# Counts of routed rows and the causal mask given to TensorE, and the turning of an expert's rows put into the down projection before it

## The reference

```python
# layer 0 attention: 16 heads of 16, key j visible from query i where j >= i
scores = jnp.where(j >= i, einsum(q, k) * attn_scale, -jnp.inf)
out = softmax(scores) @ v ; x = layernorm(x + out @ w_out + b_out)
# layer 0 experts: top 2 of 8 (the last is a no-op), at most cap = 512 rows per expert, in token order
sorted_indices = jnp.argsort(-expert_mask, axis=0)[:cap]
h = relu(einsum('ceh,ehi->cei', inputs, experts_inter))      # 7 experts, 256 -> 1024
out = einsum('cei,eih->ceh', h, experts_out) * in_w[..., None]
combined = zeros.at[used_idx].add(out) + x_flat * (noop_w * noop_mask)
# layer 1 attention: rms norm, rotary, sigmoid weights over all keys divided by their sum
# layer 1 experts: top 2 of 12 (the last 4 pass x through), silu, no cap, 256 -> 512
```

## Time and profile before

| what | value |
|---|---|
| median of three runs | 1659.26 us (1654.88 to 1662.66) |
| the profiled execution | 1661.06 us, span of its instructions 1659.5 us |
| PE, DVE, ACT, POOL busy | 83%, 55%, 42%, 30% of the span |
| one turn of layer 0 attention, mean of four | 61.9 us |
| one expert of layer 0 | 29.4 us |
| mean granted TensorE clock | 0.909 of full |

### The profile page before, as it was taken

One profiled execution on the slowest core, in us unless ns is written; L12 is line 12 of the kernel. 1 busy time (PEld: TensorE's weight loads), 2 busy tenths in 40 slices (PEclk: granted clock), 3 DMA queues, 4 the chain that ended last, 5 costly groups with the idle time before them and its releaser, 6 DMA issues.

```text
span 1659.5 us, 31170 instructions
## 1 busy us (share of the span) xinstructions
PE 1383.2 (83%) x10239; PEld 933.8 (56%) x10240; DVE 908.2 (55%) x3424; ACT 703.9 (42%) x984; POOL 495.6 (30%) x415
## 2 busy tenths in 40 slices
PE   3678898898888369999459999999998649999991
PEld 1245555555555346665325556555655448999991
DVE  1767888878886401111266766876753353434434
ACT  2145554554555111111036676767776312222223
POOL 4032344334334302122111122132312224444442
PEclk7799899999898679999779999999999769999996
DMA  6855536545513024333154647545645424444446
GB/s 168 215 107 109 116 107 133 119 111 122 120 27 116 13 71 122 107 83 83 38 113 87 121 89 149 119 93 116 133 102 148 144 85 64 71 72 71 71 63 215
DMA packets 119550, 174.71 MB, mean 105 GB/s; under 512 B 17624, under 2 KB 101618, under 8 KB 113281
## 3 DMA queue, kind: packets, MB, share of 16 engines
q1 hardware_dynamic: 96320, 148.05, 37.5%
q0 software_dynamic: 20400, 22.37, 8.6%
q10 hardware_dynamic: 2704, 2.70, 0.5%
HBM read 107.64 MB, written 72.69 MB: 109 GB/s over the span
## 4 chain that ended last, share of the span: by engine, by line
PE 55%; DVE 6%; issue 5%; ACT 4%; DMA 4%; POOL 1%; SPq 1%; POOLq 0%; DVEq 0%; ACTq 0%
PE ST L1865 7%; PE OT L769 7%; PE shared L1877 7%; PE ST L751 7%; PE ST L1324 6%; PE shared L1523 3%; PE OT L1332 3%; PE shared L1332 3%; ACT arena L890 3%; PE shared L800 3%; PE shared L1530 1%; PE shared L817 1%; DMA sum<-arena,block_to_row 1%; PE shared L781 1%; DVE scratch L1158 1%
## 5 line engine op out<-in xcount | busy, mean ns | idle before, releaser
L890 ACT ACTIVATE arena<-ST 128x1024 f32<-128x1024 f32 x416 | 412.9, 1025 | 217.9 <-PE ST L751 216.8
L751 PE MATMUL ST<-arena 96*128 96x256 bf16 (+2 forms) x1792 | 246.5, 272 | 41.8 <-DMA arena<-qk_parts 20.4
L769 PE MATMUL OT<-arena,v_aug 128*32 128x256 f32 (+1 forms) x3584 | 241.4, 384 | 5.7 <-POOL arena L1226 5.1
L751 PEld LDWEIGHTS ST<-arena 96*128 96x128 bf16 (+1 forms) x1792 | 151.0, 100 | 152.1 <-ACT arena L890 58.0
L1158 DVE CUSTOM_DVE_ANT_0 scratch<-shared,mask 128x512 bf16<-128x512 f32 (+3 forms) x293 | 135.6, 497 | 56.8 <-PE shared L865 51.8
L1972 POOL DMA_INDIRECT sum<-arena,block_to_row x71 | 111.2, 1566 | 170.9 <-DMA sum<-arena,block_to_row 118.4
L769 PEld LDWEIGHTS OT<-arena,v_aug 128*32 128x32 f32 x3584 | 92.5, 112 | 107.9 <-issue 67.4
L1877 PE MATMUL shared<-arena 128*128 x568 | 134.8, 381 | 0.0
L1226 POOL TENSOR_SCALAR_AFFINE_SELECT arena<-arena 128x512 f32<-128x512 f32 (+1 forms) x96 | 79.6, 834 | 172.2 <-ACT arena L890 172.2
L1694 POOL DMA_INDIRECT slot_x<-x_out,row_to x64 | 63.7, 995 | 165.7 <-DVE keep L1612 148.6
L1877 PEld LDWEIGHTS shared<-arena 128*128 128x128 f32 x568 | 103.0, 191 | 11.2
(11 more groups left out here) (232 smaller groups left out, 2378.8 us busy)
## 6 DMA issues: line engine op xcount, KB each, us to landing
arena<-qk_parts SPq DMA_DIRECT2D x224, 128.0 KB, 7.2
qk_parts<-qk_src SPq DMA_DIRECT2D x32, 384.0 KB, 2.6
arena<-qk_parts SPq DMA_DIRECT2D x32, 384.0 KB, 4.6
qk_parts<-qk_src SPq DMA_DIRECT2D x64, 192.0 KB, 3.0
arena<-slot_x SPq DMA_DIRECT2D x71, 130.0 KB, 2.4
arena<-qk_parts SPq DMA_DIRECT2D x32, 256.0 KB, 5.5
sum<-x_out SPq DMA_DIRECT2D x16, 512.0 KB, 3.0
arena<-in_experts_inter SPq DMA_DIRECT2D x7, 1024.0 KB, 5.1
```

The lines of the kernel that those rows point to most:

```text
L751: mm = pe.matmul(scores[:, i * 256 + at:i * 256 + at + nq], K[par][0:rows, h, kb * P:(kb + 1) * P], Q[par][0:rows, h, q0:q0 + nq], start=T ...
L769: mm = pe.matmul(OT[32 * i:32 * i + 32, q0:q0 + nq], v_aug[par][:, kb, g * GH + i, :], PT[n % RING][:, i, at:at + nq], start=(u == 0), sto ...
L890: act.activation(PT[n % RING][:, :, :], scores[:, :].rearrange("p (h n) -> p h n", h=GH), func, scale=ATT_SCALE).then_inc(L["exp"], 1)
```

## The change

The change has three parts.

1. **Counts.** `count_before` and `r_before` are gone. PE makes the counts from `r_mask` itself, in five matmuls: one with `before` over all four tiles, three with `ones_b` over the mask moved on by one, two and three tiles, and one that adds a carry from earlier sequences. VectorE sums the mask in one instruction (`count_rows`, at the start of `l3`) and adds it to the other of two carry buffers (`carry_on`). `l2` shrinks from 22 to 17 pieces in layer 0 and from 5 to none in layer 1, so that the mixed order moves by a few places.
2. **Mask.** After each fill of scores PE adds the mask on the diagonal 128 columns of every part, by a matmul of `mask_b` with the identity. VectorE then takes the maxima of the whole bank with one `tensor_reduce`; where a bank holds 384 + 128 columns it keeps four maxima by block, and `mc` gains two instructions that join them. The waits of `mx` for its own older fills and the scratch output are gone.
3. **Experts of layer 0.** The transposes for expert e+1 stand before tile 3 of the down projection of expert e. ScalarE's copy to `xgT` waits for the end of the up projection of e.

```diff
-N_ROUTE = {True: (3, 22, 11), False: (13, 5, 11)}
+N_ROUTE = {True: (3, 17, 11), False: (13, 0, 11)}
...
                 pe.wait_ge(L["rc"], k * chain_len + mask_at)
-                for t in range(TB):
-                    pe.matmul(bank[:, t * ne:(t + 1) * ne], before[:, :], r_mask[:, t, 0:ne],
-                              start=True, stop=False)
-                    mm = pe.matmul(bank[:, t * ne:(t + 1) * ne], ones_b[:, :], r_before[:, t, 0:ne],
-                                   start=False, stop=True)
-                mm.then_inc(ready, 1)
+                sums = bank[:, 0:TB * ne].rearrange("p (t e) -> p t e", t=TB)
+                pe.matmul(sums, before[:, :], r_mask[:, :, 0:ne], start=True, stop=False, skip_group_check=True)
+                for t in range(1, TB):
+                    pe.matmul(sums[:, t:TB, :], ones_b[:, :], r_mask[:, 0:TB - t, 0:ne], start=False, stop=False,
+                              skip_group_check=True)
+                pe.matmul(sums, ones_b[:, :], r_carry[k % 2][:, 0:ne].unsqueeze(1).broadcast_to([P, TB, ne]),
+                          start=False, stop=True, skip_group_check=True).then_inc(ready, 1)
...
-                            mm = pe.matmul(bank[:, at:at + S - qb * P], Q[par][0:SK, head, qb * P:(qb + 1) * P],
-                                           K[par][0:SK, head, qb * P:S], start=True, stop=True)
+                            pe.matmul(bank[:, at:at + S - qb * P], Q[par][0:SK, head, qb * P:(qb + 1) * P],
+                                      K[par][0:SK, head, qb * P:S], start=True, stop=False, skip_group_check=True)
+
+                        for _, _, at in FILLS[n % len(FILLS)]:
+                            mm = pe.matmul(bank[:, at:at + P], ident_b[:, :], mask_b[:, :], start=False, stop=True,
+                                           skip_group_check=True)
...
-        def count_before(dve, chain, ne):
-
-            yield from chain(dve.tensor_copy(r_before[:, 0, 0:ne], r_before[:, TB, 0:ne]))
-            for t in range(TB):
-                yield from chain(dve.tensor_tensor(r_before[:, t + 1, 0:ne], r_before[:, t, 0:ne], r_mask[:, t, 0:ne],
-                                        ALU.add))
+        def count_rows(dve, chain, ne):
+
+            chain.unwaited(dve.tensor_reduce(r_count[:, 0:ne], r_mask[:, :, 0:ne].rearrange("p t e -> p e t"),
+                                             AX_X, ALU.add))
+
+        def carry_on(dve, chain, ne, k):
+
+            chain.unwaited(dve.tensor_tensor(r_carry[(k + 1) % 2][:, 0:ne], r_carry[k % 2][:, 0:ne], r_count[:, 0:ne],
+                                             ALU.add))
...
-                            taken = dve.tensor_tensor_reduce(
-                                out=junk[n % 2][:, at:at + m], in0=bank[:, at:at + m], in1=mask[:, 0:m],
-                                scale=1.0, scalar=LOW, op0=ALU.add, op1=ALU.max, accum_out=mx[:, i:i + 1])
-                        taken.then_inc(free, 1)
+                        if fill == 2:
+                            dve.tensor_reduce(of_all[:, head:head + 2, 2], bank[:, :].rearrange("p (h n) -> p h n", h=2),
+                                              AX_X, ALU.max).then_inc(free, 1)
+                        elif fill % 3 == 0:
+                            dve.tensor_reduce(of_all[:, head + fill // 3:head + fill // 3 + 1, 0], bank[:, :].unsqueeze(1),
+                                              AX_X, ALU.max).then_inc(free, 1)
+                        else:
+                            dve.tensor_reduce(mx_blocks[:, head + fill // 3, :],
+                                              bank[:, :].rearrange("p (b n) -> p b n", n=P),
+                                              AX_X, ALU.max).then_inc(free, 1)
...
+                        chain.unwaited(dve.tensor_reduce(of_all[:, heads, 1], mx_blocks[:, heads, 0:3], AX_X, ALU.max))
+                        chain.step(dve.tensor_copy(of_all[:, heads, 3], mx_blocks[:, heads, 3]))
...
                 for t in range(TB):
+                    if t == TB - 1 and e + 1 < E0:
+                        turn_rows(e + 1)
...
         def b_act(act):
             def emit(e, par, half):
+                wait(act, b_up, e * MI)
```

More of the change, by code:

```diff
@@ L522, in build @@
         scratch = sb("scratch", [P, S])
-        junk = [scratch[:, i * (S // 2):(i + 1) * (S // 2)].bitcast(BF16) for i in range(2)]
+        mask_b = sb("mask_b", [P, P], BF16)
         mx = sb("mx", [P, NH * TB])
+        mx_blocks = sb("mx_blocks", [P, NH, TB])
         mx_rest = sb("mx_rest", [P, NH * TB])
@@ L541, in build @@
         r_mask = sb("r_mask", [P, TB, NEM], BF16)
-        r_before = sb("r_before", [P, TB + 1, NEM], BF16)
+        r_carry = [sb(f"r_carry{i}", [P, NEM], BF16) for i in range(2)]
+        r_count = sb("r_count", [P, NEM])
         row_to = [sb(f"row_to{i}", [P, TB, 2], I32) for i in range(2)]
@@ L1083, in a_route_dve @@
                 yield from chain(dve.tensor_tensor(r_mask[:, :, 0:ne], oh[0], oh[1], ALU.add))
-                yield from count_before(dve, chain, ne)
                 assert chain.n == MASK0, chain.n
@@ L1161, in emit @@
-                        taken.then_inc(free, 1)
-                    elif step == "mc":
-                        for i in (2, 1):
-                            banks.read(dve, turn, ("mx", (n + 1) * HALF_MX - i))
-                        chain = Chain(dve, L["mchain"], k * 8 + 4 * n)
+                        of_all = mx[:, :].rearrange("p (h b) -> p h b", b=TB)
+                        fill, head = n % len(FILLS), n // len(FILLS) * 2
+                        if fill == 2:
[8 more added lines that the diff above has]
+                                              AX_X, ALU.max).then_inc(free, 1)
+                    elif step == "mc":
+                        for b in range(banks.n):
+                            banks.read(dve, turn, ("mx", max(i for i in range(n * HALF_MX, (n + 1) * HALF_MX)
+                                                             if banks.place[turn.kind][("mx", i)][0] == b)))
+                        chain = Chain(dve, L["mchain"], k * 12 + 6 * n)
+                        heads = slice(n * HH, (n + 1) * HH)
+                        of_all = mx[:, :].rearrange("p (h b) -> p h b", b=TB)
+                        chain.unwaited(dve.tensor_reduce(of_all[:, heads, 1], mx_blocks[:, heads, 0:3], AX_X, ALU.max))
+                        chain.step(dve.tensor_copy(of_all[:, heads, 3], mx_blocks[:, heads, 3]))
@@ L1597, in c_route_dve @@
                 chain.n = MASK1
+                count_rows(dve, chain, ne)
                 dve.wait_ge(L["ex"], k * 2 + 2)
@@ L1843, in d_pe @@
             pe.wait_ge(LC["oe"], NB * NG)
-            pe.matmul(shared[0][:, 0:E1], ones_b[:, :], r_before[:, TB, 0:E1], start=True, stop=True
+            pe.matmul(shared[0][:, 0:E1], ones_b[:, :], r_carry[NB % 2][:, 0:E1], start=True, stop=True
                       ).then_inc(d_cnt, 1)
```

43 lines of the change are left out of this document (18 added, 25 removed).

## The result

The changed kernel takes 1663.68 us (median of 20 runs, 1658.4 to 1670.74) where the kernel before takes 1659.24 us (20 runs, 1653.31 to 1665.03). The ratio is 1.0029, with a 95% interval from 1.0017 to 1.0041. Run a second time, beside other kernels on one chip, it is 1.0024 (1.0007 to 1.0041). So the change costs 4 us, inside the 0.5% that were to be called no change, where 9 us of gain were forecast.

The account below looks back on a forecast made before the run. PE was taken to lead about 47 us of a layer 0 middle turn, VectorE about 15. Terms of -8.4, -0.9, -3.0, +15, -7.2 and -4.5 sum to -9.0 us: 1650 us (1643 to 1658; outer range 1634 to 1667).

Parts of the forecast that it names:

- counts, with the stall and the three ends: Six layer 0 turns -8.4 us, one slow count instruction -0.9, three uncovered last turns (two in layer 1) -3.0.
- masks and clock: Layer 0 attention: PE's added mask matmuls on the path +15 us, PE's clock falling less often -7.2 us.
- turned rows: Layer 0 experts: moved transposes remove PE's 0.74 us wait for ScalarE's copies at six borders, -4.5 us.
- order: Order of steps in the turns shifts by a place or so: 2 us either way, nothing in the sum.
- outer range of 1634 to 1667 us: Whole kernel: the forecast's wide range, leaving out the slow rival and the tail below the clock's.
- I had written 0.3: End of layer 1: sign that the row from mask to `ps` takes under 0.3 us.
- +15: Layer 0 attention: of 32 us of mask matmuls, 2.0 us a turn on the path, ends 6 and 32.
- 0.6 us a turn, in one stretch: VectorE-led stretch of a layer 0 turn: gain from cheaper whole-bank fills, 7 of which count there.
- PE pays for every mask: Rival, layer 0 attention: all 32 us of masks on the path, clock brings nothing; 1674 us, chance 0.12.
- The wait moves and the clock stays: Rival, layer 0 turns: the forecast without the clock's 7 us; 1657 us, no change, chance 0.2.
- the length of a turn: Sign in layer 0's middle turns: a turn near 61.5 us.
- A turn over 63 us at a clock of 0.92 would prove the masks mis-sized: Sign in layer 0's middle turns: a turn that long would mean the masks' cost was wrongly sized.

Follow-up runs that it names:

- e15: The changed kernel as it is, run again beside others on one chip: 1662.80 us, 1.0024 of the kernel before.
- e13: The changed kernel with 17 l2 steps, each weighted 0.25 x 22/17 so the sum of weights stays that of 22: 1642.92 us, 0.9902 of the kernel before.
- e6: The kernel before with the new counts alone, but 22 steps kept for l2 in layer 0: 0.9931 of the kernel before.
- e2: The kernel before with the masks alone (PE adds them, VectorE reduces whole banks): 1658.38 us, 0.9990 of the kernel before.
- e9: The changed kernel with 22 l2 steps and no masks on PE, maxima by VectorE's masked parts: 1666.09 us, 0.9903 of the kernel before.
- e11: The changed kernel with 22 l2 steps, without mask matmuls, VectorE reducing whole banks of unmasked scores: 1655.84 us, 0.9850 of the kernel before.
- e3: The kernel before with only the layer 0 experts' transposes moved into the down projection: 1652.00 us, 0.9964 of the kernel before.
- e7: The kernel before with only the number of l2 steps in layer 0 changed, 17 instead of 22: 1.0118 of the kernel before.
- e1: The kernel before with the new counts alone, 17 l2 steps in layer 0: 1678.21 us, 1.0116 of the kernel before.
- e4: The whole change without the masks, maxima by VectorE's masked parts as before: 1667.68 us, 1.0060 of the kernel before.
- e16: The changed kernel with two projections moved one place ahead in the body turns: 1658.77 us, 1.0003 of the kernel before.
- e10: e9 plus PE's mask matmuls with a mask of zeros, VectorE keeping its masked parts: 1674.42 us, 0.9957 of the kernel before.
- e5: The whole changed kernel with 22 steps kept for l2 in layer 0 instead of 17: 1668.40 us, 0.9890 of the kernel before.
- e12: The changed kernel with 27 steps for l2 in layer 0 instead of 17: 0.9950 of the kernel before.
- e17: e13 without the mask matmuls, VectorE reducing whole banks of unmasked scores: 0.9931 of the kernel before.

## Why the prediction was wrong, point by point

**The step that failed** is one sentence of the sum: "The order of steps in the turns also shifts by a place or so; I give that 2 us either way." It was a guess with no row behind it, and the runs give it 1.2% in the kernel before and 1.2 to 1.4% in the changed kernel, 20 to 23 us, all of it a loss. In its place the runs show PE waiting for the exponential where the shifted order leaves too little work in front of a block of scores: 12.4 us of such waits in the middle turns of e15, 3.2 in e13 with the weights kept. The waits for the exponential stood in the earlier trace rows, and the order of both kernels could be read; laid side by side, st by st, they show the thin places. I had used these waits only as cover for the masks.

The other terms, against what was measured:

| term | predicted, us | measured, us |
|---|---|---|
| counts, with the stall and the three ends | -8.4 - 0.9 - 3.0 = -12.3 | -11.6 (e6, 0.69% of 1684), in part in other places |
| masks and clock | +15 - 7.2 = +7.8 | -0.2 (e2); +8.3 for PE's and -10.3 for VectorE's half (e9 to e11) |
| turned rows | -4.5 | -6.6 (e3) |
| order | 0, 2 either way | +22 (e7 less before), +20 (e15 less e13) |

Without the order the sum should have been about -18; e13 gives -16. That the forecast of -9 lay near the measured +4 at all, inside the outer range of 1634 to 1667 us, is luck: the other terms promised 9 us too little, and the order, put at nothing, took 20.

**Counts.** Right in kind and in the sum. The wait moved to `oT`, 2.8 us a turn (over 2 was forecast), and at the end of layer 1 PE's first count matmul starts 0.36 us after the mask does (the first row is VectorE's mask), where before the last sum ended 1.2 us behind the mask's start. I had written 0.3:

```profile
1335.44 0.21 DVE L1613 TENSOR_TENSOR r_mask<-r_oh 128x48 bf16<-128x48 f32 x1
...
1335.80 0.20 PE L827 MATMUL shared<-r_mask,before 128*128 128x48 bf16 x1 [3.48 <-DVE r_mask L1613]
```

Where the gain lies was partly wrong. In layer 1 attention the prediction gave the counts nothing. Every profiled kernel with the new counts takes 428.0 to 430.2 us there (after, e1, e4, e13 to e16), and the three with the old ones 431.7 to 432.7 (before, e2, e3), all on chips where the kernel before takes 1659 us: some 3 us. In the middle turns of layer 0, where 5.6 us were forecast, e13 takes 244.8 us and e2, with the old counts and the same masks, 246.5, a difference too small for two profiles. So that the sum fits so well is luck in part.

**Masks.** The pace was right: a second mask follows the first by some 0.06 us (0.22 us for one, 0.28 for two, in the rows of 239 to 241 us above). The wrong term was the part on the path, +15: it is 8.3 in e10, with what the clock gives back in it. Fills on VectorE were right by instruction, 0.68 us lasting and 0.60 to the next (forecast 0.69 and 0.61), and wrong in place: I counted 0.6 us a turn, in one stretch, and e9 less e11 is 10.3 us in all.

```profile
267.23 0.68 DVE L1168 TENSOR_REDUCE mx<-shared 128x1 f32<-128x512 f32 x1
...
267.83 0.15 DVE L1114 SCALAR_TENSOR_TENSOR keep<-r_s 128x4 f32<-128x4 f32 x1
```

**Clock.** It rose from 0.92 to 0.95 in the middle turns, 12.7 us of full rate against 19.8 (254.93 x 0.05 and 247.40 x 0.08), 1.8 us a turn where I had 1.2. The prediction named two causes, a wait less at `ps` and more work on PE. On one chip the masks alone give 0.95 (e2), the counts alone 0.90 (e1) and the old layer 0 attention 0.91 (e3), so it is the second. One run doesn't fit: e9, which has no masks on PE, has 0.95 too.

**Experts.** An expert's period is 28.43 us, from 697.41 to 725.84, against 29.43; the up projection takes 13.73 us instead of 14.00 besides the 0.74 of the wait:

```profile
697.41 13.73 PE ST L1345 x32
711.15 6.91 PE shared L1355 x32
718.05 3.45 PE OT L1355 x16
721.51 0.87 PE shared L1333 x8
722.38 3.46 PE OT L1355 x16
725.84 13.73 PE ST L1345 x32
```

**Rivals.** "PE pays for every mask" gave the sign that came, by a cause that e2 and e10 refute. "The wait moves and the clock stays" gave the class that came, no change; the wait did move, but the clock rose. Of the signs to look for, those on the counts, the reductions, the masks, the clock and the experts came out, but for the 0.36 us above; the length of a turn didn't. "A turn over 63 us at a clock of 0.92 would prove the masks mis-sized" would have misled: the turn is 63.7 us, and kept weights bring it to 61.2 with all masks in place. No sign was set on the waits for the exponential, and that is where the time was.

## What to carry to other kernels

When an edit changes the number of steps that a planner spreads, the whole list behind it moves: compare the two orders between each pair of blocks that feed another engine, and price each place that falls short of that engine's time, with what the moved steps issue on that engine too. Keep the sum of weights when instructions are merged or removed (here 0.25 x 22/17; e13), and only then judge the edit itself. An edit that seems to cost or bring nothing (the masks, 0.9990) may be two large effects that cancel; a run with each half alone shows them.

## What the hardware showed besides

Work added to PE was in part paid back by the clock. On one chip, the middle turns of e3 take 243.8 us at a clock of 0.91; those of e2, with the masks on PE (14.6 us more matmuls, an estimate from 57 ns each) and VectorE's whole-bank reductions, take 246.5 us at 0.95. In all profiled kernels with the masks on PE the clock there is 0.93 to 0.96, in those without 0.90 to 0.93, e9 with 0.95 left out. In a stretch where PE waits often and its clock drops behind the waits, its busy time is no measure of what an added matmul costs.

A VectorE instruction with two SBUF inputs was held up in front of the new sum: in each of the four middle turns one `qk_rest` (L1148) takes 1.40 us instead of the 0.69 of the earlier trace rows, beside a GpSimd instruction that reads SBUF.

```profile
262.62 0.69 DVE L1168 TENSOR_REDUCE mx<-ST 128x1 f32<-128x512 f32 x1
263.23 1.40 DVE L1148 TENSOR_TENSOR qk_rest<-qk_flat,qk_src 128x512 f32<-128x512 f32 x1
264.55 0.68 DVE L1171 TENSOR_REDUCE mx_blocks<-ST 128x4 f32<-128x512 f32 x1
...
265.75 0.19 DVE L1049 TENSOR_REDUCE r_count<-r_mask 128x8 f32<-128x32 bf16 x1
```

```profile
262.99 1.10 POOL L1244 TENSOR_SCALAR_AFFINE_SELECT arena<-arena 128x1024 f32<-128x1024 f32 x1 [0.94 <-ACT arena L897]
265.37 1.16 POOL L1232 TENSOR_TENSOR qk_src<-qk_rest,qk_src 128x512 bf16<-128x512 f32 x1 [1.29 <-ACT qk_src L929]
```

This agrees with the Trainium skill, SBUF — State Buffer, section Who interferes with whom, by which an instruction with two SBUF inputs contends with a GpSimd instruction that reads SBUF and a `tensor_reduce` doesn't. The new sum (L1049), a `tensor_reduce` from SBUF, lasts 0.19 us in the middle of such an instruction (L1232); the reductions of a bank read PSUM and are no test. I had used that rule on the small count instructions and not on this one, which lies in VectorE's row up to `oT`. What the 0.7 us cost the turn wasn't tried.

Chips gave the kernel before 1659 to 1661 us or 1683 to 1684 us. Layer 1 attention of the changed kernel, the same instructions, takes 428 to 430 us on the chips of the result and of e13 to e16, and 436 to 440 us on those of e5 and e9 to e12. It takes 436 us also in e17, on a chip where the kernel before takes 1661 us. On the two slow chips the middle turns of seven of the eight profiles hold 3.9 to 10.8 us in which PE waits for nothing that the trace shows, elsewhere 0.9 us at most. Why stays open; it is the reason for reading ratios only.
